# Cross-attention and FFN on one core: both transpositions of a head pair ahead of the next scores, other homes and times for small loads, no alignment of the code

## What is computed

```python
# x, ctx: (16, 64, 512); bias: (16, 32, 64, 64); Wq, Wk, Wv: (512, 4096); Wo: (4096, 512)
q, k, v = layernorm(x) @ Wq, ctx @ Wk, ctx @ Wv            # 32 heads of 128
p = softmax(where(mask, q @ k.T / sqrt(128) + bias, -inf))
x = x + (p @ v) @ Wo
z = layernorm(x)
w = top-8 of softmax(z @ router_W.T + router_b), summed by mapped expert
x = x + z @ base_W.T + base_b + 2 * sum_e(w_e * (z @ A_e.T) @ B_e.T)
```

## Time and profile before

| | |
|---|---|
| median of 3 runs | 790.44 us (788.65 to 790.91) |
| the profiled execution | 791.96 us |
| its span | 790.1 us |
| PE's matmuls, weight loads | 780.8 us (99%), 652.0 us (83%) |
| DVE | 521.5 us (66%) |
| ACT | 399.9 us (51%) |
| POOL | 185.3 us (23%) |
| DMA | 118.40 MB, 150 GB/s |
| mean granted clock of PE | 0.998 |

### The profile page before, as it was taken

How to read it: one execution, slowest core, us unless ns; L and a number is a source line. 1 busy time by engine, 2 the same in 40 slices (tenths; PEclk the granted TensorE clock), 3 DMA queues, 4 the chain that set the end, 5 groups by cost and what they waited for, 6 DMA issues and landing times.

```text
span 790.1 us, 16795 instructions
## 1 busy us (share of the span) xinstructions
PE 780.8 (99%) x6360; PEld 652.0 (83%) x6360; DVE 521.5 (66%) x951; ACT 399.9 (51%) x1138; POOL 185.3 (23%) x203
## 2 busy tenths in 40 slices
PE   8999999999999999989999999999999999999998
PEld 7888888888888888878888888888888888887886
DVE  6883626267677665577666776676667676657974
ACT  5663525246556555573665456535654466435520
POOL 0225041024333434232222122212211221010200
PEclk9999999999999999999999999999999999999999
DMA  6536773245544547583564355534563355342002
GB/s 226 199 121 220 225 243 138 109 139 159 190 160 159 169 154 215 171 250 111 164 182 135 110 157 161 163 110 130 162 177 115 112 160 176 109 118 83 2 6 103
DMA packets 108078, 118.40 MB, mean 150 GB/s; under 512 B 44239, under 2 KB 77007, under 8 KB 107998
## 3 DMA queue, kind: packets, MB, share of 16 engines
q1 hardware_dynamic: 107998, 117.31, 47.7%
HBM read 81.64 MB, written 35.65 MB: 148 GB/s over the span
## 4 chain that ended last, share of the span: by engine, by line
PE 93%; DMA 2%; DVE 2%; SPq 1%; issue 1%; ACT 0%
PE pY L1393 42%; PE pP L1393 39%; PE pY L1552 4%; PE pO L1577 2%; PE pT_ L1577 2%; PE pS L1562 1%; DMA wv_raw<-in_L_xattn_Wv 1%; PE pO L1393 1%; PE pT_ L1562 1%; DMA v<-v_hbm 1%; DMA k_hbm<-stage 1%; SPq L425 1%; DVE st L980 1%; PE pS L1577 1%; DVE y L1129 0%
## 5 line engine op out<-in xcount | busy, mean ns | idle before, releaser
L1129 DVE TENSOR_TENSOR y<-y,pY 128x512 f32<-128x512 f32 x124 | 84.6, 682 | 24.6 <-PE pY L1393 24.2
L1393 PE MATMUL pY<-wo_hi,oT_hi 128*128 128x512 f32 x248 | 97.4, 393 | 1.2 <-issue 1.2
L1393 PE MATMUL pY<-wo_lo,oT_hi 128*128 128x512 f32 x248 | 97.2, 392 | 0.0
L1393 PE MATMUL pY<-wo_hi,oT_lo 128*128 128x512 f32 x248 | 97.2, 392 | 0.0
L910 DVE TENSOR_TENSOR wk_lo<-wk_raw,wk_hi 128x256 fp32r<-128x256 f32 x96 | 46.7, 487 | 62.2 <-ACT wk_hi L651 61.3
L759 ACT ACTIVATE pr<-pr,mx 128x64 f32<-128x64 f32 x256 | 86.2, 344 | 2.8 <-DVE mx L1146 2.8
L651 ACT CAST wk_hi<-twk 128x256 fp32r<-128x256 f32 x128 | 50.7, 409 | 64.5 <-PE pP L1393 53.6
L1393 PE MATMUL pP<-xo_hi,wk_hi 128*128 128x512 f32 x196 | 78.1, 399 | 0.0
L1393 PE MATMUL pP<-xo_hi,wk_lo 128*128 128x512 f32 x196 | 76.6, 391 | 0.0
L1393 PE MATMUL pP<-xo_lo,wk_hi 128*128 128x512 f32 x196 | 76.4, 390 | 0.0
L584 POOL TENSOR_TENSOR bias<-bias,madd 128x512 f32<-128x512 f32 x32 | 41.5, 1308 | 148.2 <-DMA bias<-in_fside_Bx32xSxS 148.2
(11 more groups left out here) (282 smaller groups left out, 1896.6 us busy)
## 6 DMA issues: line engine op xcount, KB each, us to landing
v_hbm<-stage SPq DMA_DIRECT2D x64, 256.0 KB, 2.3
k_hbm<-stage SPq DMA_DIRECT2D x64, 256.0 KB, 3.6
k<-k_hbm SPq DMA_DIRECT2D x16, 1024.0 KB, 5.1
v<-v_hbm SPq DMA_DIRECT2D x16, 1024.0 KB, 7.0
wk_raw<-in_L_xattn_Wk SPq DMA_DIRECT2D x16, 512.0 KB, 4.4
wo_raw<-in_L_xattn_Wo SPq DMA_DIRECT2D x16, 512.0 KB, 3.7
bias<-in_fside_Bx32xSxS SPq DMA_DIRECT2D x128, 64.0 KB, 3.6
wk_raw<-in_L_xattn_Wq SPq DMA_DIRECT2D x16, 512.0 KB, 4.7
```

The source lines that it names most:

```text
L1129: nc.vector.tensor_tensor(y[:, t, :], y[:, t, :], src[:, :], ALU.add).then_inc(y_added, 1)
L1393: mm = nc.tensor.matmul(bank_, a, b, start=first and n == 0, stop=last and n == len(terms) - 1, skip_group_check=read_between)
```

## The change

`turn_p(h + 1)` moves ahead of the scores in the loop and in the last pair but one. v of the first pair gets a home of its own, v0, in R0 (free after product (QA, 4)), and is loaded behind that product and ahead of the last `store` and of `load_wk`; the wait for the puts moves to the load of pair 1. a_raw, r_raw, b_raw and bw_raw get homes in R0 as well and are loaded in iterations 2, 3 and 4; bb, rb and mapi in iteration 1, and DVE's work on mapi goes from iteration 0 to 3. Both `addr_align` go. In the last pairs ACT has `exp(h + 2, 0)` behind the `o_high`, and `ffn_weights(4)` and (5) with their `split_ffn` go one place later. `make_c21(QB)` goes ahead of `lower_wo(0)`. At the start two of 14 transpositions are replaced by 26 of 32x32.

```diff
--- before.py
+++ after.py
@@ -143,6 +143,12 @@
         oT = [at(f"oT_{part}", R0 + 8192 * n, [P, 2, T], F32R) for n, part in enumerate(("hi", "lo"))]
         wo = [[at(f"wo_{part}{i}", R0 + 32768 + 8192 * i + 4096 * n, [P, 2, D], F32R)
                for n, part in enumerate(("hi", "lo"))] for i in range(2)]
+
+        v0 = at("v0", R0 + 16384, [P, NT, 2 * DH])
+        a_raw = at("a_raw", R0 + 16384, [P, D])
+        r_raw = at("r_raw", R0 + 18432, [NR, D])
+        b_raw = at("b_raw", R0 + 20480, [P, DC, ER])
+        bw_raw = at("bw_raw", R0 + 24576, [P, DC, D])
         r0 = R0 + 49152
         bb = at("bb", r0, [P, D])
         onehot = at("onehot", r0 + 2048, [P, E, NR])
@@ -170,7 +176,6 @@
         xT_hi = at("xT_hi", R1, [P, DC, T], F32R)
         xT_lo = at("xT_lo", R1 + 16384, [P, DC, T], F32R)
         fw = [at("fw_hi_", R1 + 32768, [P, DC, D], F32R), at("fw_lo_", R1 + 40960, [P, DC, D], F32R)]
-        bw_raw = at("bw_raw", R1 + 49152, [P, DC, D])
 
 
         R2 = 114688
@@ -192,9 +197,6 @@
         pr = [at(f"pr{i}", R4 + 8192 + 2048 * i, [P, NB, S]) for i in range(2)]
         pT = [at("pT0", R4 + 12288, [P, NT, S]), at("pT1", R4 + 6144, [P, NT, S])]
         wk_raw = [at(f"wk_raw{i}", R4 + 16384 + 4096 * i, [P, DC, 2 * DH]) for i in range(2)]
-        a_raw = at("a_raw", R4 + 16384, [P, D])
-        r_raw = at("r_raw", R4 + 18432, [NR, D])
-        b_raw = at("b_raw", R4 + 20480, [P, DC, ER])
 
         b12 = [at("b12_hi", R4 + 16384, [P, 2, HALF], F32R), at("b12_lo", R4 + 20480, [P, 2, HALF], F32R)]
 
@@ -432,7 +434,7 @@
                 sp.dma_start(k[:, :, :], k_hbm[2 * i:2 * i + 2].rearrange("h p t -> p h t")).then_inc(ld_k, 16)
 
             def load_v(i):
-                sp.dma_start(v[:, :, :], v_hbm[i // 2, :, :, i % 2 * 2 * DH:(i % 2 + 1) * 2 * DH]
+                sp.dma_start((v if i else v0)[:, :, :], v_hbm[i // 2, :, :, i % 2 * 2 * DH:(i % 2 + 1) * 2 * DH]
                              .rearrange("t p n -> p t n")).then_inc(ld_v, 16)
 
             def store(n, i, made_):
@@ -501,15 +503,11 @@
                 load_bias(h)
             store(QA, 3, c22_made)
             store(QA, 1, c12_made)
+
+            sp.wait_ge(prod, DONE[QA, 4])
+            load_v(0)
+            store(QA, 2, c21_made)
             load_wk(QA - 9)
-            store(QA, 2, c21_made)
-            sp.wait_ge(prod, DONE[QA, 4])
-            sp.dma_start(bb[:, :], base_b.partition_broadcast(P)).then_inc(ld_small, 16)
-            sp.dma_start(rb[:, :], router_b.partition_broadcast(P)).then_inc(ld_small, 16)
-            sp.dma_start(mapi[:, :], emap.partition_broadcast(P)).then_inc(ld_small, 16)
-            for i in range(4):
-                sp.wait_ge(put[0][i], 16 * (QA // 2 + 1))
-            load_v(0)
             for i in range(NP - 1):
                 sp.wait_ge(wo_l, i + 1)
                 load_wo(i + 1)
@@ -522,16 +520,20 @@
                 if i + 24 < NSET:
                     load_wk(i + 24)
                 sp.wait_ge(o_full, 4 * (i + 1))
+                if i == 0:
+                    for n in range(4):
+                        sp.wait_ge(put[0][n], 16 * (QA // 2 + 1))
                 load_v(i + 1)
-                if i == NP - 4:
-
-                    sp.wait_ge(w_lo[5], NSET - 1)
-                    sp.wait_ge(tw_made, 4 * (NSET - 1))
+                if i == 1:
+                    sp.dma_start(bb[:, :], base_b.partition_broadcast(P)).then_inc(ld_small, 16)
+                    sp.dma_start(rb[:, :], router_b.partition_broadcast(P)).then_inc(ld_small, 16)
+                    sp.dma_start(mapi[:, :], emap.partition_broadcast(P)).then_inc(ld_small, 16)
+                if i == 2:
                     sp.dma_start(a_raw[:, :], a_d).then_inc(ld_a, 16)
                     sp.dma_start(r_raw[:, :], router_W).then_inc(ld_a, 16)
-                if i == NP - 3:
-                    sp.wait_ge(prod, len(ORDER))
+                if i == 3:
                     sp.dma_start(bw_raw[:, :, :], bw_d).then_inc(ld_ffn, 16)
+                if i == 4:
                     for o in range(DC):
                         sp.dma_start(b_raw[:, o, :].rearrange("p (e r) -> p e r", e=E), b_d[:, o]
                                      ).then_inc(ld_ffn, 16)
@@ -858,11 +860,11 @@
             h = 2 * (NP - 2)
             turned_p(h)
             turned_p(h + 1)
-            exp(h + 2, 0)
             o_high(h, 0)
             o_high(h, 1)
             o_high(h + 1, 0)
             o_high(h + 1, 1)
+            exp(h + 2, 0)
             exp(h + 2, 1)
             split_ffn(0)
             exp(h + 3, 0)
@@ -871,14 +873,14 @@
             split_ffn(2)
             split_ffn(3)
             wo_high(NP - 1)
-            split_ffn(4)
             turned_p(h + 2)
             turned_p(h + 3)
-            split_ffn(5)
+            split_ffn(4)
             o_high(h + 2, 0)
             o_high(h + 2, 1)
             o_high(h + 3, 0)
             o_high(h + 3, 1)
+            split_ffn(5)
             split_ffn(6)
 
             for i in range(NT + 1):
@@ -1206,8 +1208,8 @@
             weights(1)
             lower_w(w2, 3)
             lower_w(w2, 4)
+            make_c21(QB)
             lower_wo(0)
-            make_c21(QB)
             lower_w(w2, 5)
             lower_w(w2, 6)
 
@@ -1245,7 +1247,7 @@
                 add_tile(i, 6)
                 lower_of(w, 6)
                 add_tile(i, 7)
-                if i == 0:
+                if i == 3:
                     dve.wait_ge(ld_small, 48)
                     nc.vector.tensor_copy(mapf[:, :], mapi[:, :]).then_inc(msk, 1)
                     dve.wait_ge(msk, 2)
@@ -1463,10 +1465,10 @@
                     turn(xn[:, m % NX, :], first_turn(j))
                     turn(xn[:, (m + 1) % NX, :], second_turn(j))
 
-            def warm_up(count):
+            def warm_up(count, n=P):
 
                 for _ in range(count):
-                    nc.tensor.transpose(pY[1][:, 0:P], ident[:, :], ident[:, :])
+                    nc.tensor.transpose(pY[1][0:n, 0:n], ident[0:n, 0:n], ident[0:n, 0:n])
 
             pe.wait_ge(made, 1)
             cols0 = tile_cols(0)
@@ -1483,7 +1485,9 @@
 
             warm_up(8)
             turn_ctx(0, first_turn(0))
-            warm_up(14)
+            warm_up(12)
+
+            warm_up(26, 32)
             turn_ctx(1, first_turn(1))
 
             pe.wait_ge(w_lo[0], 1)
@@ -1575,7 +1579,7 @@
                         for i in range(2):
                             rows = slice(64 * i, 64 * i + 64)
                             mm = nc.tensor.matmul(pO_of[s][i][64 * d:64 * d + 64, t * S:(t + 1) * S],
-                                                  v[rows, t, s * DH + 64 * d:s * DH + 64 * d + 64],
+                                                  (v if h >= 2 else v0)[rows, t, s * DH + 64 * d:s * DH + 64 * d + 64],
                                                   pT[s][rows, t, :], start=True, stop=True)
                             if t == NT - 1 and d == 1:
                                 mm.then_inc(o_full, 1)
@@ -1642,8 +1646,6 @@
             times(n, 4)
             for p in (2, 6, 7, 5):
                 times(QB, p)
-
-            nc.tensor.addr_align(256, offset=142)
             times(QB + 1, 1)
             times(QB, 3)
             times(QB, 4)
@@ -1652,17 +1654,12 @@
                 n = QA + 2 + i
                 h = 2 * i
                 turn_p(h)
+                turn_p(h + 1)
                 scores(h + 2)
                 scores(h + 3)
-                turn_p(h + 1)
                 times_v(h)
                 times_v(h + 1)
-                for p in (1, 2) if i else (2,):
-                    times(n, p)
-                if i % 3 == 2:
-
-                    nc.tensor.addr_align(256, offset=18)
-                for p in (6, 7):
+                for p in (1, 2, 6, 7) if i else (2, 6, 7):
                     times(n, p)
                 times_wo(i, 0)
                 times_wo(i, 1)
@@ -1691,13 +1688,12 @@
             ffn_weights(3)
             for t in range(4, NT):
                 times_wo(i, t)
-                if t == 5:
-                    ffn_weights(4)
             turn_p(h + 2)
             turn_p(h + 3)
-            ffn_weights(5)
+            ffn_weights(4)
             times_v(h + 2)
             times_v(h + 3)
+            ffn_weights(5)
             ffn_weights(6)
 
             def turn_last(t):
```

## The result

The changed kernel takes 787.06 us (median of 8, 785.60 to 788.15) against 790.13 for the kernel before in the same session (median of 8): ratio 0.9956, 95% interval 0.9944 to 0.9969, so 2.4 to 4.4 us less. It is faster, as forecast, and inside the range; but of the 6.0 us forecast, 3.1 to 3.5 came. The profiled execution took 787.0 us (span 785.2), its own median.

What follows compares the result with a forecast made beforehand. PE, busy 99% of the span, was taken as the bound. Gains of 2.1 (shape) + 1.1 (first iteration) + 0.1 (code) + 2.7 (tail) = 6.0 us took 790.4 to 784.4 us, range 782.0 to 787.5.

Steps and rivals of the forecast that it cites:

- What bounds the kernel: Whole kernel: PE is busy 99% of the span; only its work, idling between instructions and clock count.
- Both transpositions first: Loop over head pairs: fewer shape changes save 0.15 us an iteration, 2.1 us in all (0 to 4.3).
- First iteration: Iteration 0: 2.97 us leave PE, 1.9 come back as a wait for c11, 1.1 stays (0 to 2.97).
- Code: Instruction fetch outside iteration 0: stalls some 1.1 us before, 1.0 after, so 0.1 us gained (bounds -1.1 and +12).
- Last pairs: Tail: 0.7 us less idling, 1.55 no clock fall, 0.45 FFN transpositions moved; together 2.7 us (1.1 to 2.9).
- Start: Warm-up and first products: 26 narrow transpositions replace two wide ones, forecast 0 us (up to +1.8).
- Rival 1: Last pairs: the clock still falls, 784.4 + 1.55 = 786.0 us; chance 0.15.
- Rival 2: Loop without fillers: code stalls at two borders in eight iterations make it slower, 797.3 us; chance 0.07.
- Rival 3: Loop: the changes of shape give nothing, 784.4 + 2.1 = 786.5 us; chance 0.13.
- Rival 4: Iteration 0: c11 is not late, 784.4 - 1.9 = 782.5 us; chance 0.08.

Runs made afterwards that it cites:

- last pairs alone: Kernel before with only the change's edits to TensorE, ACT and DVE from pair 14 on: 788.75 us, ratio 0.9978.
- loads alone: Kernel before with only the homes and times of the loads taken over (SP's order, v0, other homes, masks in iteration 3): 788.47 us, ratio 0.9977.

## Why the prediction was right, and where it was wrong

- **What bounds the kernel** held: all that moved the time was on PE's timeline.
- **Both transpositions first**: 0.15 us an iteration forecast, 0.18 measured, in every kernel that has the order. Right, and `o_low` and c11 kept up.
- **First iteration**: 1.1 us (1.25 with the shape change of iteration 1) forecast, 1.4 measured by the means of the table (1.0 to 1.8 by pairs of profiles). The 2.97 us left PE exactly (7.98 to 5.01). Of the 1.9 forecast to come back, 1.4 to 1.6 did (25.58 and 25.76 us to the end of V of iteration 1, against 24.18 with the new order and no such wait). `lower_wo(0)` took 1.22 us instead of the 1.7 I copied from its row, so c11 was earlier than forecast; and I did not follow DVE past c11, to `add_tile(0,0)`, which `times_wo(0,2)` waits for. I also read c21 first as a gain: alone it is a loss of 1.0 us in the trace. The stall for code of iteration 0, which I let fall into the wait for c11, had gone through the 48 slots of the new warm-up.
- **Code**: this is the step of the mechanism that failed. The places were right, double borders in 3, 6, 9, 12 with a stall and in 7, 10, 13 without. The size was not: "1.1 before, 1.0 after, so 0.1 us" against 1.27 or 0.49 before and 2.3 after. I took the drift of 12 slots as what sets the stall and left the moment at which the sequencer enters the block as the old order had it. But with both transpositions ahead, V comes at the same time or sooner, and the block before it is entered later: in the loop's 16 late double borders of four kernels in the old order (before twice, last pairs alone, loads alone) the V excess averages 0.24 us, in 32 of eight profiles in the new order 0.55 (the changed kernel with the old warm-up, with its borders elsewhere, is left out: 3.33 us in all), and the packets of the blocks begin 1.01 us before V in the one and 0.63 in the other. The Trainium skill (Advanced Engine Details and Errata, ISA Cache) says "Only 2 cache lines!", beside 128 KB for TensorE; by the rule of two lines the stall must come at the second border of a dense stretch, and the traces agree: none over 0.1 us was seen where T to V holds one border.
- **Last pairs**: 2.7 us forecast, 2.8 in the trace. Right in all three terms for an execution in which the clock falls, and the cause of the fall was read well enough to remove it: none in 51. But here a second step failed, by as much as the first. The forecast was made against a profiled execution 1.5 us above the median and took "the same difference off the median", while 1.55 of its 6.0 us was a fall that only 13 of 58 executions have. The median gains the 1.15 of the order, not the 2.7; the lowest bound, 1.1, was the right value for it.
- **Start**: 0 forecast (up to +1.8), +0.8 measured in T0, of which the warm-up at the lower clock is up to 0.65. I had priced the passes and not asked at which clock they would run.
- **Rivals**: Rival 1 (the clock still falls) did not come, though its 786.0 us is what the forecast should have said of a median that has no fall to lose. Rival 2 (slower by code) named the right mechanism at too high a price: its stalls came to 0.55 us on average, not 0.99, at four places and not eight. Nor was the first stall dear because its fetch met a busy DMA queue, as was said for it: that packet took 1.02 us, less than the 1.28 of iteration 3, but began 0.84 us after the first pass of V(0), where that of iteration 3 began 0.96 before. Rival 3 gave the right time (786.5) for the wrong reason: the shape changes gave their 2.4 us, and the code took 1.4 of it. Rival 4 fell: c11 was late.

The sum again with measured terms: 2.4 (shape) + 1.2 (first iteration) - 1.4 (code) + 2.8 (tail) - 0.8 (start) = 4.2, and 2.6 where the clock did not fall before either. That the measured 3.1 to 3.5 us lie inside the range is in part luck: the terms that failed are 1.55 for the clock, 1.5 for the code and 0.8 at the start, and the range was wide enough for rivals that had other causes.

## What to carry to other kernels

When an edit reorders work on an engine that runs dense, short instructions, ask not only where the code borders fall but when the sequencer enters each block, relative to the first instruction of the next: an order that is better for the array can be worse for the fetch. Any edit ahead of such a stretch, a warm-up of 24 instructions included, moves all borders behind it, so single parts can't be judged by the time alone; and an alignment is only as good as the distance it happens to fill. Before moving a helper step behind an urgent one, look whether the engine idles in front of the urgent one. And where the profiled execution lies above the median, ask first which of its costs the median does not have: the mean clock of the other executions told it here.

## What was not expected of the hardware

- A filler for the alignment takes 71 to 84 ns on TensorE's sequencer (13 in 0.85 to 1.01 us from the first one's start to the last one's, 230 in 17.0), while a load and matmul of V take 16 ns together. Behind queued 512-column products 22 of them cost about 0.1 us and 13 between 0 and 0.3; behind scores 16 cost 0.67.
- The stall at one and the same slot is not a constant: 0.0 to 0.38 us in iteration 6 in four executions of the old order, and 0.52 to 0.82 in iteration 6 of four executions with the changed kernel's code positions. It goes with when the block's packet begins (1.22 us before V to 0.03 after it) and how long it takes (0.88 to 1.42 us); why the packet begins when it does stays open.
- The fall of the clock to 1.2 GHz in pair 14 came in three profiled executions and not in a fourth with the same TensorE work and the same 0.65 us of idling; by the mean clock it is in 13 of 58 executions of one and the same program. The DMA share of the stretch was 0.76 to 0.88 with the fall and 0.27 without, but 0.95 and 0.77 in two others that also kept 2.4 GHz. So the DMA share does not tell, and with the idling gone it came in none of 51; what decides within the old order stays open.
- The same 128x1024 subtraction on DVE (`lower_wo(0)`) takes 1.76 or 1.77 us in all five kernels with the old times of the loads, and 1.21 or 1.22 in all with the new ones, in either order on DVE. The 1.76 came only where POOL worked at the same time (5 of 224), and POOL's addition beside it took 1.53 us instead of 0.74.
